# Products with V of the masked attention layer, issued in groups of eight tiles at three fixed places

## The reference

```python
scores = jnp.einsum('bqhd,bkhd->bhqk', q, k)
scores = scores + jnp.einsum('bqr,bkr->bqk', q_rope, k_rope)[:, None]
scores = scores / scale
scores = jnp.where(causal[None, None], -jnp.inf, scores)
w = jax.nn.softmax(scores, axis=-1)
attn = jnp.einsum('bhqk,bkhd->bqhd', w, v).reshape(Bb, Tt, D_MODEL)
return attn @ W_o
```

## Time and profile before

| | us |
|---|---|
| median of 3 runs (2759.8 to 2767.98) | 2766.81 |
| span of the profiled execution, first to last instruction | 2676.7 |
| TensorE busy | 2323.5 (87%) |
| VectorE busy | 1899.1 (71%) |
| ScalarE busy | 1773.8 (66%) |
| GpSimd busy | 890.3 (33%) |
| the V products (L1139), busy | 756.1 |

### The profile page before, as it was taken

How to read it: one execution, slowest core, us unless ns; L and a number is a source line. 1 busy time by engine, 2 the same in 40 slices (tenths; PEclk the granted TensorE clock), 3 DMA queues, 4 the chain that set the end, 5 groups by cost and what they waited for, 6 DMA issues and landing times. The chain is left out here.

```text
span 2676.7 us, 44214 instructions
## 1 busy us (share of the span) xinstructions
PE 2323.5 (87%) x15891; PEld 902.8 (34%) x15970; DVE 1899.1 (71%) x3300; ACT 1773.8 (66%) x3759; POOL 890.3 (33%) x1317
## 2 busy tenths in 40 slices
PE   4789989888988998998999999988989988988954
PEld 3222223222322344454444444322223323422424
DVE  6779987878797567656566666787986687697520
ACT  4288877766766666555656656578877777777741
POOL 5450132363254337327415114032023223214124
PEclk7699999999999999999999999999999999999977
DMA  4241103212313421440332122112113312311314
GB/s 161 94 131 28 36 23 107 55 48 85 94 33 100 140 65 58 119 134 24 121 103 70 47 81 68 42 38 68 27 30 114 91 32 85 111 40 54 115 32 169
DMA packets 137888, 205.50 MB, mean 77 GB/s; under 512 B 21130, under 2 KB 104426, under 8 KB 137494
## 3 DMA queue, kind: packets, MB, share of 16 engines
q1 hardware_dynamic: 119238, 141.52, 18.0%
q0 software_dynamic: 17536, 59.58, 7.3%
q10 hardware_dynamic: 896, 1.56, 0.2%
HBM read 138.52 MB, written 60.54 MB: 74 GB/s over the span
## 5 line engine op out<-in xcount | busy, mean ns | idle before, releaser
L1311 ACT ACTIVATE PB<-bank 128x512 f32<-128x512 f32 (+3 forms) x2944 | 1438.0, 556 | 565.8 <-PE bank L999 294.9
L1499 DVE TENSOR_REDUCE small<-unit 128x1 f32<-128x1024 f32 x1024 | 1210.9, 1219 | 243.0 <-PE unit L1019 233.5
L1019 PE MATMUL unit<-RK 61*128 61x512 bf16 (+4 forms) x2762 | 871.0, 375 | 129.3 <-DVE small L1499 74.4
L1139 PE MATMUL bank<-PB,VP 128*32 128x512 f32 (+3 forms) x5888 | 756.1, 567 | 13.4 <-ACT PB L1311 7.8
L999 PE MATMUL bank<-RK 64*128 64x512 bf16 x2048 | 678.2, 387 | 73.6 <-ACT PB L1311 39.9
L1496 DVE CUSTOM_DVE_ANT_0 unit<-unit,maskb 128x640 f32<-128x640 f32 (+7 forms) x512 | 387.6, 770 | 245.7 <-PE unit L1019 228.9
L1019 PEld LDWEIGHTS unit<-RK 61*128 61x128 bf16 (+1 forms) x2816 | 211.4, 95 | 560.2 <-DVE small L1499 230.2
L999 PEld LDWEIGHTS bank<-RK 64*128 64x128 bf16 x2048 | 154.2, 94 | 506.0 <-ACT PB L1311 324.3
L995 PE MATMUL bank<-RK 128*128 128x256 bf16 (+2 forms) x960 | 275.4, 296 | 1.7 <-issue 0.5
L994 PE MATMUL bank<-RK 128*128 128x256 bf16 (+3 forms) x935 | 264.5, 294 | 12.1 <-ACT PB L1311 4.8
L1765 POOL CAST small<-small 128x8 bf16<-128x8 f32 x128 | 24.8, 194 | 621.1 <-DVE small L1499 572.8
(11 more groups left out here) (197 smaller groups left out, 1961.4 us busy)
## 6 DMA issues: line engine op xcount, KB each, us to landing
RK<-qk_parts SPq DMA_DIRECT2D x128, 192.0 KB
qk_parts<-SC SPq DMA_DIRECT2D x48, 384.0 KB, 2.6
RK<-rqk_parts SPq DMA_DIRECT2D x48, 384.0 KB
qk_parts<-SC SPq DMA_DIRECT2D x48, 256.0 KB, 3.0
RK<-qk_parts SPq DMA_DIRECT2D x128, 96.0 KB
XSB<-x_sorted SPq DMA_DIRECT2D x38, 192.0 KB, 4.7
y_sorted<-XSB SPq DMA_DIRECT2D x38, 192.0 KB, 2.1
qk_parts<-SC SPq DMA_DIRECT2D x48, 128.0 KB, 2.9
```

The source lines that it names most:

```text
L1019: p = e.matmul(unit[k // 2 - 2][:, c0:c1], slot(L, u, 0, 0, rows)[:, 128 * qt:128 * qt + 128], slot(L, u, 1, 0, rows)[:, c0:c1], start=Tru ...
L1139: p = e.matmul(bank[k][32 * j:32 * j + 32, c0:512], VP[:, 8 * (pr // 8) + kt, 9 * h:9 * h + 32], prob(L, t)[:, c0:512], start=(kt == 0), s ...
L1311: e.activation(prob(L, t)[:, c0:512], bank[k][:, c0:512], ACT.Exp, scale=LAYERS[L].scale).then_inc(bank_free[k], 1)
L1499: e.tensor_reduce(m, unit[k // 2 - 2][:, :], AX.X, ALU.max, negate=True).then_inc(bank_free[k], 1)
```

## The change

In the masked layer the planner's early `av` rule (L679) holds only for `av` 6 of a pair; the other six are put in two at a time, inside the `score` step of tiles 8 and 9 (`av` 0 and 1), of 16 and 17 (2 and 3) and of 24 and 25 (4 and 5), behind its matmuls. For these three steps the loop at L666 is skipped, so the exponentials of tiles 8, 9, 16, 17, 24 and 25 now wait for an `av` step that is issued behind their own scores. The planner books the time of the step's exponentials after the two `av` steps. The other two layers keep their rule.

```diff
@@ score(h)
         pe = P.at["PE"]
+        scored = []
...
-                before = tile_group(L, t, NPB)
-                ready = max(pe, av_end[before] if before is not None else 0.0)
-                P.free[k] = tile_end[L, t] = P.spend("ACT", ready, 0.07 + (512 - c0) / 970)
+                scored.append((t, k, c0, pe))
...
         P.at["PE"] = pe
+        if paired(h):
+            av()
+            av()
+        for t, k, c0, pe in scored:
+            before = tile_group(L, t, NPB)
+            ready = max(pe, av_end[before] if before is not None else 0.0)
+            P.free[k] = tile_end[L, t] = P.spend("ACT", ready, 0.07 + (512 - c0) / 970)
+
+    def paired(h):
+
+        if not 0 <= h < len(halves):
+            return False
+        L, t = halves[h]
+        return LAYERS[L].causal and t % LAYERS[L].n2 in (8, 16, 24)
+
+    def alone(L, gg):
+
+        return not LAYERS[L].causal or gg % (LAYERS[L].n2 // 4) == 6
@@ the loop over h
-            while need is not None and need not in av_end:
+            while need is not None and need not in av_end and not paired(h):
                 av()
...
-            elif to_av and all((to_av[0][0], 4 * to_av[0][1] + i) in tile_end for i in range(4)) and \
+            elif to_av and alone(*to_av[0]) and all((to_av[0][0], 4 * to_av[0][1] + i) in tile_end for i in range(4)) and \
```

## The result

The change made the kernel slower. In the runs of the comparison the kernel before took 2763.06 us (median of 7 runs) and the changed one 2779.39 us (2772.32 to 2787.42, 7 runs): ratio 1.0053, 95% interval 1.0034 to 1.0072, some 15 us more by that ratio, where I had forecast 15 us less.

The account below looks back on a forecast made before the run. TensorE's queue was taken as the bound; seams 18.2 and sends 2.4, less bumps 4.8 and 1 us for DMA-set ends, net some 15 us: span 2661.7 plus 90.1 gave 2752 us, range 2741 to 2766.

Parts of the forecast that it names:

- What bounds the kernel: Masked layer: TensorE's queue sets the time, busy 716.60 of 784.00 us; time leaving it is gain if VectorE and ScalarE follow.
- The seam: Between two joined `av` steps: tail and lead go, .19 us a join, 18.2 us for 96 seams.
- high end: Upper bound for the 96 seams: the whole .24 of a group's lead, tail and seam is saved, 23.0 us.
- Who is moved: Order in a masked pair: only `av` 0, 2 and 4 move, each past two `score` steps; the others stay.
- (a) the gate: At the joins, six exponentials wait for an `av` behind their scores; no stall, 1.0, .7 and .7 us to spare.
- (b) bunching: Scores run closer together between joins, thinnest at tiles 18 to 25; .05 us a pair there, .05 for tile 16.
- (c) VectorE's maxima: Tiles 8 and 9: .05; first head's cut moves ahead, so the .45 wait at 14 and 15 does not arise.
- (d) the sends: Two `send` steps a pair: the first costs 0 ahead of tile 12, the second saves .15 in about 16 pairs, 2.4 us.
- The sum: Whole kernel: seams 18.2 and sends 2.4, less bumps 4.8 and 1 for DMA-set ends; net 14.8, say 15 us.
- Side work dealt out differently: Rival, chance .12: fewer `beside` turns shift side-work chains; half lands at 2735 to 2755, half at 2758 to 2785.
- ScalarE's gate: Rival, chance .09: waiting exponentials idle ScalarE and delay side copies TensorE needs; 2771 to 2792, most likely 2778.
- The 90.1 us: Time around the profiled span at the median, added to span 2661.7 to forecast 2751.8.

Follow-up runs that it names:

- joined lists: Kernel before's step list with V products (`av`) moved to the three joins per masked pair, side work left in place; all 96 joins: ratios 1.0005 to 1.0020.
- joined_only: Kernel before's list with only `av` groups 0 to 5 moved behind scores of tiles 8/9, 16/17, 24/25; 2773.99 us, ratio 1.0019 to before.
- joined_cut: Kernel before's list with all joins, plus the first head's cut of maxima behind the first join; 2771.95 us, ratio 1.0020 to before.
- side_only: Changed kernel's list with joins undone, `av` groups at fixed separate places; side work, sends, first head's cut kept; 2778.13 us, 1.0049 to before.
- side_again: Changed kernel's list with joins undone, new places of side work, sends and first head's cut kept, rerun in a short session; ratio 1.0041 to before.
- after_turns: Changed kernel with one more side-work turn ahead of six `score` steps of each masked pair, joins kept; ratio 1.0014 to before.

## Why the prediction was wrong, point by point

**What bounds the kernel.** Right: TensorE's queue. What I read past is that side work puts ScalarE's copies into that queue's path, and that V products were what TensorE did meanwhile.

**The seam.** Right in kind, a little too small: .24 a join (2.00 less 1.86, and a lead of .10) where I took .19. That is the high end, 23.0 us for 96. The Trainium skill's rule that a change of tiling mode drains TensorE (TensorEngine Tiling (Array Packing), Key Properties) gave the same high end if all of lead, tail and seam is drain, and the trace agrees with that reading. An undisturbed pair took 19.70 us where I had forecast 19.95. In the joined lists a join is worth .14 net, 13.7 us for 96, because the first `send` costs .25 there.

**Who is moved.** Not quite right. In before, beside side work, `av` 1, 3 and 5 stand one `score` step earlier in 5, 4 and 1 of the 32 pairs, and `av` 0, 2 and 4 in 7, 9 and 4, so more groups move than I wrote.

**(a) the gate, (b) bunching.** (a) is right as far as undisturbed pairs go: 1.58 and 1.18 us of ScalarE idle, no bank late for it. Twelve buffers changed nothing that can be measured. The .10 us of (b) were too much: such a pair shows some .04 of small waits that before lacks.

**(c) VectorE's maxima.** Mostly right: the cut stands ahead and the .45 for the scores of 14 and 15 does not arise. But joined_only, with the cut left where it was, has the same 20.08 us as joined_cut, and its unit of tiles 14 and 15 waits .09 behind the `send`, so moving the cut was not what saved those .45.

**(d) the sends.** Right, as booked: the first costs nothing ahead of tile 12, since the wait at tile 13 falls by .26, and the second saves its .15 inside the join. What the place is worth shows against joined_cut, which differs from the changed kernel in an undisturbed pair only in where the first `send` stands, and takes 20.08 us instead of 19.70.

**The sum.** It counted each of 96 joins at the price of an undisturbed pair, and a new distribution of the side work at nothing. These are the two steps that failed. Joined in the old list, all 96 gave 1.0005 to 1.0020 and not a gain of 13.7 us: half of them, 49, take away cover from a side step, and these cost 7 us net instead of saving 7. On top of that the changed list is 5 us (short sessions) to 9 us (the ratios of the first comparison and of joined_cut) slower than the joined list, although its undisturbed pairs are .38 faster. The text named who is moved past what among scores, sends and cuts, and left out the side steps, which stand in 22 of 32 pairs.

**Side work dealt out differently.** The mechanism was among my rivals with .12. Its slower half reached from 2758 to 2785, and the 2779.39 lie in it; I had taken either direction for as likely. Its size is not isolated: side_only and side_again lose 11 to 14 us, of which up to 7.7 may be the `send`'s. One part was shown in its rows (3.1 us and the lower clock beside it in pair 14, 4 to 5 us). In the list of before, side steps were in places where V products covered them and where fetches were on time; I had that list in the trace and did not ask what a displacement would do to it.

**The slower rival.** "ScalarE's gate" forecast 2771 to 2792 and the time lies in it by luck: with the gate removed its waits stayed.

**The time around the span.** The 90.1 us were a difference of sessions and not of what lies around the span (1.8 us). It did not move the forecast difference, but it hid that the trace and the median were of different sorts.

**Open.** What makes a session long or short was not looked into. Nor was the rest of the loss of side_again taken apart wait by wait (5.4 us for W of GpSimd in pair 8, 3.4 us for a maximum in pair 10), and no run has the new side work with the sends where before has them. The two short-session ratios of the change and of after_turns can't be told apart.

## What to carry to other kernels

Before moving work that is ready early, ask what it was hiding where it stood; count each move by its neighbours, not by the quiet stretch in which it is easiest to measure. Where a planner's list changes, compare the two lists step by step, and split an edit by one criterion from the old list: here 41 of 96 moves gave 9 us and the others took them away. And look at what else an edit of the list leaves in a new place: one small product between two others cost .24 us a pair in a run that was meant to show something else. A queue in order that carries both stores and fetches (SyncE here) turns a late producer of a store into a late fetch.

## What the runs showed of the hardware that I had not expected

- The same program takes 2675 or 2765 us by session (or chip), with the masked layer 7.6 us longer and the other layers 33 to 36 us longer each. In layer 0 the mean granted clock was .98 and .96 and TensorE's busy time 752.7 and 765.8 us, so most of the 36 us there are waits.
- A `send` of 128 columns costs TensorE .25 us by itself between bf16 products over all 128 columns, and nothing inside a step of V products.
- A wait of TensorE that grows from .39 to 1.23 us at the start of pair 30 was followed by 6.8 us at half the clock (granted .50), in each of five profiles. A wait's price was then well above its own length.
